# A transformer layer on one core: two loads and three groups of small products moved, and the inverse's equal iterations as a loop on TensorE

## What is computed

```python
q_l = q.reshape(b, H, M, l, DH).sum(axis=3) / l        # M = 64 landmarks
k_l = k.reshape(b, H, M, l, DH).sum(axis=3) / l
attn1 = softmax(q @ k_l^T); attn2 = softmax(q_l @ k_l^T); attn3 = softmax(q_l @ k^T)
z = attn2^T / (max(col) * max(row))                    # Moore-Penrose inverse, 6 iterations
for _ in range(6):
    az = a @ z
    z = 0.25 * z @ (13 * I - az @ (15 * I - az @ (7 * I - az)))
out = attn1 @ z @ (attn3 @ v)
```

## Time and profile before

| | |
|---|---|
| median of 3 runs | 1166.59 us |
| the profiled execution's own time | 1159.38 us |
| its span | 1157.6 us |
| PE busy | 1100.6 us, 95% of the span |
| DVE, ACT, POOL busy | 634.0, 303.0, 300.5 us |
| PE, share of the chain that ended last | 87% |
| PE busy in 300 to 400 us | 85.75 us |
| granted clock of TensorE, mean | 0.99 |
| DMA, mean over the span | 60 GB/s |

### The profile page before, as it was taken

How to read it: one execution, slowest core, us unless ns; L and a number is a source line. 1 busy time by engine, 2 the same in 40 slices (tenths; PEclk the granted TensorE clock), 3 DMA queues, 4 the chain that set the end, 5 groups by cost and what they waited for, 6 DMA issues and landing times.

```text
span 1157.6 us, 22799 instructions
## 1 busy us (share of the span) xinstructions
PE 1100.6 (95%) x9162; PEld 914.3 (79%) x9162; DVE 634.0 (55%) x1346; ACT 303.0 (26%) x457; POOL 300.5 (26%) x298
## 2 busy tenths in 40 slices
PE   4998999999988899999999999889999999999996
PEld 4887888888877756677766777777888888899996
DVE  6467566555467566676686686663332333334442
ACT  4432233332223422342332333231111111111110
POOL 6000000000200013235534544552323323334343
PEclk9999999999999999999999999899999999999999
DMA  9200000000220030211321324145333333231221
GB/s 338 107 1 1 1 1 1 1 1 1 57 77 5 4 146 28 102 55 65 139 65 64 102 74 142 61 135 115 51 52 46 51 52 51 33 48 35 44 27 12
DMA packets 48551, 69.13 MB, mean 60 GB/s; under 512 B 7872, under 2 KB 41792, under 8 KB 47424
## 3 DMA queue, kind: packets, MB, share of 16 engines
q1 hardware_dynamic: 34720, 47.50, 12.9%
q0 software_dynamic: 13296, 16.92, 8.6%
q10 hardware_dynamic: 432, 3.24, 0.7%
HBM read 42.10 MB, written 26.46 MB: 59 GB/s over the span
## 4 chain that ended last, share of the span: by engine, by line
PE 87%; DVE 6%; issue 3%; POOL 2%; ACT 1%; another core or an unknown queue 0%; POOLq 0%; DVEq 0%
PE ps L1712 20%; PE ps L1735 10%; PE ps L1599 10%; PE ps L1375 9%; PE ps L1638 9%; PE ps L1336 9%; PE ps L1630 5%; PE ps L1509 2%; PE ps L1695 1%; PE ps L1618 1%; PE ps L1310 1%; PE ps L1490 1%; PE ps L1477 1%; PE ps L1390 1%; PE ps L1566 1%
## 5 line engine op out<-in xcount | busy, mean ns | idle before, releaser
L1712 PE MATMUL ps<-mem 128*128 128x256 f32 (+1 forms) x1504 | 260.7, 329 | 0.0
L1712 PEld LDWEIGHTS ps<-mem 128*128 128x128 f32 x1504 | 232.7, 191 | 21.5
L565 POOL DMA_INDIRECT out<-mem x71 | 122.9, 1732 | 255.8 <-DVE mem L1215 189.1
L1735 PE MATMUL ps<-mem 128*128 x568 | 135.3, 381 | 5.7 <-DVE mem L1207 3.4
L1207 DVE TENSOR_TENSOR mem<-mem,ps 128x512 f32<-128x512 f32 x71 | 48.8, 687 | 164.6 <-PE ps L1712 143.8
L535 POOL TENSOR_TENSOR mem<-mem,small 128x1024 f32<-128x1024 f32 x36 | 68.6, 1906 | 260.7 <-DVE small L1144 127.8
L1599 PE MATMUL ps<-mem 128*128 128x512 f32 x288 | 129.7, 594 | 1.3 <-DVE mem L1028 1.3
L771 ACT ACTIVATE mem<-ps 128x512 f32<-128x512 f32 x71 | 42.4, 597 | 319.3 <-PE ps L1712 312.8
L1638 PE MATMUL ps<-mem 128*128 128x256 f32 x512 | 120.0, 388 | 0.0
L1375 PE MATMUL ps<-mem 128*128 128x256 f32 x512 | 119.1, 386 | 0.8 <-ACT mem L645 0.8
L1735 PEld LDWEIGHTS ps<-mem 128*128 128x128 f32 x568 | 104.3, 191 | 18.5 <-issue 6.3
(11 more groups left out here) (219 smaller groups left out, 1314.7 us busy)
## 6 DMA issues: line engine op xcount, KB each, us to landing
mem<-w_gu SPq DMA_DIRECT2D x9, 1024.0 KB, 4.3
mem<-xs_d SPq DMA_DIRECT2D x22, 260.0 KB, 2.8
mem<-x SPq DMA_DIRECT2D x8, 512.0 KB, 7.4
mem<-x SPq DMA_DIRECT2D x32, 128.0 KB, 2.1
out<-mem SPq DMA_DIRECT2D x32, 128.0 KB, 1.7
mem<-w_down SPq DMA_DIRECT2D x8, 512.0 KB, 5.1
xnt_d<-mem ACTq DMA_DIRECT2D x3, 1056.0 KB, 5.4
mem<-xnt_d SPq DMA_DIRECT2D x3, 1056.0 KB, 4.9
```

Of the source, the lines that this page charges most:

```text
L565: pool.indirect_dma_start(out=out_rows, out_offset=bass.IndirectOffsetOnAxis(ap=rows[:, D + 1:D + 2].bitcast(U32), axis=0), in_=ys[:, r % ...
L1712: mm = pe.matmul(bank(2 * c + n % 2)[:, i * size:(i + 1) * size], w[:, k, c, f * P:(f + 1) * P], xst[:, a % 2, k, 0:size], start=(k == 0), ...
L1735: mm = pe.matmul(bank(down_bank(a, b))[:, 0:D], hid[:, u, i * size + b * P:i * size + (b + 1) * P], w_d_s[:, e, f], start=(f == 0), stop=( ...
```

## The change

It has four parts.

1. The two moves of loads. `e3s[0]` and `e3s[3]` swap places, so that `wfc` now shares its space with `e3s[0]`, last used at m = 12. SP issues `w_fc` once 13 of the `c1_ut` are done, ahead of the band. `batch_columns(1)` goes behind the gate and up weights of the four experts.
2. The small work of attention 2 is moved to later m, on all three engines: `sim2(2)` and `sim2(3)` with their wait for `b_sub` from m = 1 to 2, `a_transposed` from m = 2 and 3 to 4 and 5, the two sums from m = 5 to 6 and the scale from 7 to 9 (the first sum stays at 4).
3. The 64 first products (line 1456) go from m = 14 to m = 15.
4. PE's part of the inverse: the first pair is written out in `first_pair`, the ten pairs n = 2 to 20 become five trips of a loop in hardware (`pe.Fori`) with two pairs in its body, and the pair n = 22 follows. Counts of semaphores in the loop are register values, so each wait is an instruction of its own (`wait_alone`). Waits that follow from others are left out: a pair now has 5 waits, each an instruction of its own; before, it had 6 such instructions, and four products carried a wait besides. DVE's and ACT's programs for the inverse are as before.

```diff
-        e3s = [at(a, RT * 2 * P).rearrange("p (t c) -> p t c", t=RT) for a in (o + J * D, SQ, wk_at, o)]
+        e3s = [at(a, RT * 2 * P).rearrange("p (t c) -> p t c", t=RT) for a in (o, SQ, wk_at, o + J * D)]
...
+            sp.wait_ge(s("c1_ut"), NP2 - 3)
+            sp.dma_start(wfc, w_fc.rearrange("(j p) c -> p j c", p=P)).then_inc(s("w_in"), 16)
             sp.wait_ge(s("c1_sim"), 2 * NP2)
             sp.dma_start(band, conv_band.rearrange("h p c -> p h c")).then_inc(s("band_in"), 16)
             sp.dma_start(bfc, b_fc.rearrange("(o c) -> o c", o=1).to_broadcast([P, D])).then_inc(s("bfc_in"), 16)
             for m in range(XR):
                 residual_rows(m)
-            sp.wait_ge(s("c1_v3mm"), NP2)
-            sp.dma_start(wfc, w_fc.rearrange("(j p) c -> p j c", p=P)).then_inc(s("w_in"), 16)
             sp.wait_ge(s("a_xnt_out"), 16 * (B - 1))
-            batch_columns(1)
             sp.wait_ge(s("p_wt_mm"), NQ // 4)
             for e in range(4):
                 expert_gate_up(e)
+            batch_columns(1)
...
-                if m == 1:
-                    pe.wait_ge(s("c1_utb"), 1)
+                if m in (2, 4, 5):
+                    pe.wait_ge(s("c1_utb"), m)
+                    pe.wait_ge(s("c1_v3"), 2 * m - 2)
+                if m == 2:
                     sim2(2)
                     sim2(3)
-                if m in (2, 3):
-                    pe.wait_ge(s("c1_utb"), m)
-                    pe.wait_ge(s("c1_v3"), 2 * m - 2)
-                    a_transposed(2 * m - 4)
-                    a_transposed(2 * m - 3)
+                if m in (4, 5):
+                    a_transposed(2 * m - 8)
+                    a_transposed(2 * m - 7)
                 if more:
                     c1_sim(2 * m + 5)
-                if m == 1:
+                if m == 2:
                     pe.wait_ge(s("b_sub"), B)
-                if m in (2, 3):
-                    pe.wait_ge(s("b_at_act"), m - 1)
-                    pe.wait_ge(s("b_at_dve"), m - 1)
-                if m == NP2 - 2:
+                if m in (4, 5):
+                    pe.wait_ge(s("b_at_act"), m - 3)
+                    pe.wait_ge(s("b_at_dve"), m - 3)
+                if m == NP2 - 1:
                     pe.wait_ge(s("c1_raw"), 2 * NP2)
...
-            for n in range(0, 4 * ITERS, 2):
+            def first_pair():
+                for k in range(2):
+                    pe.wait_ge(s("i_yw"), k + 1)
+                    for i in range(8):
+                        mm = square(k, i)
+                    mm.then_inc(s("i_squaremm"), 1)
+                c1_v3(NP2 - 1)
+                for k in range(2):
+                    pe.wait_ge(s("i_br"), k + 1)
+                    if k == 0:
+                        pe.wait_ge(s("i_yw"), 4)
+                    for i in range(8):
+                        mm = cube(k, i)
+                    mm.then_inc(s("i_cubemm"), 1)
+
+            def pair(n, done):
+
                 for k in range(4):
-                    if n == 0 and k == 2:
-                        c1_v3(NP2 - 1)
-                    (square_ready if k < 2 else cube_ready)(n + k % 2)
-                    if n >= 2 and k % 2 == 0:
-                        next_ready(n - 2 + k // 2)
+                    if k < 2:
+                        wait_alone(pe, "i_yw", done + n + k + 1)
+                        if k == 0:
+                            wait_alone(pe, "i_factor", done + n - 1)
+                    else:
+                        wait_alone(pe, "i_br", done + n + k - 1)
                     for i in range(8):
                         mm = (square if k < 2 else cube)(n + k % 2, i)
-                        if n >= 2:
-                            crossed = next_values(n - 2 + k // 2, 8 * (k % 2) + i)
+                        crossed = next_values(n - 2 + k // 2, 8 * (k % 2) + i)
                     mm.then_inc(s("i_squaremm" if k < 2 else "i_cubemm"), 1)
-                    if n >= 2 and k % 2 == 1:
+                    if k % 2 == 1:
                         crossed.then_inc(s("i_nextmm"), 1)
+
+            first_pair()
+            pe.wait_ge(s("i_w0"), 1)
+            pe.wait_ge(s("c1_r3"), NP2)
+            pe.wait_ge(s("c1_v3"), NQ)
+            with pe.Fori(0, ITERS - 1) as it:
+                pair(2, 4 * it)
+                pair(4, 4 * it)
+            pair(4 * ITERS - 2, 0)
```

More of the change, by code:

```diff
@@ L672, in _ @@
                     c1_raw(2 * m + 4)
-                if m == 1:
+                if m == 2:
                     sim2_exp(2)
                     sim2_exp(3)
-                if m in (2, 3):
-                    b = 2 * (m - 2)
+                if m in (4, 5):
+                    b = 2 * (m - 4)
                     act.wait_ge(s("b_at_tp"), b + 1)
@@ L949, in _ @@
                     c1_first_max(m + 2)
-                if m == 1:
+                if m == 2:
                     sim2_less_max(2)
                     sim2_less_max(3)
-                if m in (2, 3):
-                    b = 2 * (m - 2) + 1
+                if m in (4, 5):
+                    b = 2 * (m - 4) + 1
                     dve.wait_ge(s("b_at_tp"), b + 1)
@@ L970, in _ @@
                     dve.tensor_reduce(zz[:, 0:1], mx2, AX, ALU.max).then_inc(s("b_sums"), 1)
-                if m == 5:
+                if m == 6:
                     dve.wait_ge(s("b_at_dve"), 2)
@@ L975, in _ @@
                     dve.tensor_reduce(zz[:, 1:2], sm2s, AX, ALU.max).then_inc(s("b_sums"), 1)
-                if m == 7:
+                if m == 9:
                     dve.wait_ge(s("b_gmax"), 1)
```

## The result

| | before | change |
|---|---|---|
| median, first comparison | 1167.37 us (1164.97 to 1168.68, 4 runs) | 1151.8 us (1146.11 to 1153.58, 4 runs) |
| ratio of medians | | 0.9865, interval 0.9836 to 0.9893 |
| median, second comparison, another chip (`e10` below) | 1159.23 us (11 runs) | 1145.87 us (1144.63 to 1146.23, 4 runs) |
| ratio | | 0.9882, interval 0.9858 to 0.9906 |

The change is faster, by 15.6 us in one comparison and 13.4 in the other; both intervals lie clear of 1. The forecast was 12.8. In the profiled execution of the changed kernel (1153.58 us) the gain is smaller, 5.8 us of 1159.4. Where the rest was lost is shown further down.

What follows compares the result with a forecast made beforehand. PE bounds the kernel, and in the inverse the arrival of its instructions does. Terms -4.0 - 0.75 - 2.8 - 5.2 = -12.8 us: 1146.6 from the profiled 1159.4, 1153.8 against the median 1166.6; 8-in-10 range 1148 to 1182.

Steps and rivals of the forecast that it cites:

- `sim2` to m = 2: First stage, m == 1: removes PE's 4.0 us wait at line 1365, with some 1.5 us new idling at `c1_max_columns(3)`; -4.0 us.
- gone: 5.20 - 3.65 of slow matmuls after it: First stage, m == 1: the 16 matmuls after the removed stall return to usual speed, 1.55 us won.
- `a_transposed`: First stage, m == 2, 3 to 4, 5: same PE work where PE has no gap, copies fit others' idling; 0.
- First products: End of first stage, line 1456: moved to m == 15, the 64 products fill PE's wait for bank 6; -0.75 us.
- they cover it: End of first stage: the products' 3.88 us hide the 0.75 us wait for bank 6 between two `c1_ut`.
- Loads: Inverse: earlier `w_fc` and later columns remove the 3.09 us stall (-2.3) and slow matmuls after it (-0.5); -2.8 us.
- The loop: Inverse: kept instruction blocks spare fetch stalls, 1.1 us a trip over four trips plus one stall of 0.8; -5.2 us.
- The next bound: Inverse loop: VectorE at 8.3 us a trip limits the gain to 3.0 us a trip, -12 in all.
- Rival A: Inverse loop: branch finds its target gone, four blocks fetched each trip, 15.8 us instead of 11.3; 1179 us, chance 0.33.
- Rival B: Inverse loop: blocks are fetched again at each edge, pace stays 3.6 us a block, only moves count; 1159 us, chance 0.12.
- rival C: Moves give nothing (4 us wait returns at `c1_max_columns(3)`), register steps eat the loop's gain; 1163 to 1167 us, chance 0.05.
- What was to be seen: Signs: 4 or 5 loop packets, not 14; copies 9.6 to 10.4 us per four; no 3 us inverse stall.

Runs made afterwards that it cites:

- e10: The changed kernel itself, unaltered, timed again on another chip beside the kernel before: 1145.87 us, ratio 0.9882.
- e4: The changed kernel with `sim2(2)`, `sim2(3)` and the wait for `b_sub` back at m = 1, on all engines: one run, 1148.6 us against 1159.5 before.
- e1: The changed kernel with the inverse written out as before, so the moves without the loop: 1153.73 us against 1159.9 before, ratio 0.9948.
- e6: The changed kernel with `w_fc` and the columns of batch 1 loaded where they were before: one run, 1148.06 us.
- e7: The changed kernel with four pairs in the loop's body, two trips, and two pairs written out behind it: one run, 1147.57 us.
- e5: The changed kernel with the 64 first products back at m = 14: one run, 1144.14 us.
- e8: The changed kernel with six pairs in the loop's body, two trips, and seven iterations of the inverse instead of six (two pairs more work): 1171.15 us.
- e2: The changed kernel with the same pairs and 5 waits a pair, written out by a Python loop instead of the hardware loop: 1156.37 us, ratio 0.9972 to before.
- e9: The changed kernel with half of `c1_ut(1)` ahead of `c1_max_columns(3)`, and at m = 2 the scores ahead of `c1_max_rows(3)`: 1145.5 us, ratio 0.9881 to before.
- e11: The same kernel as e9, timed again beside the changed kernel on one chip: 1147.04 us, ratio 0.9892 to before.
- e3: The kernel before with the hardware loop alone, no moves: 1151.6 us, ratio 0.9927 to before.

## Why the prediction was right, term by term

The forecast was -12.8 us. The marks give -11.9 (the change) and -12.7 (e10) at the start of the landmark values, the medians -13.4 and -15.6. The terms are less good than the sum, whose closeness is in part luck: the two terms in c1 were 2.4 us too large together (4.75 for 2.3) and the loop's about 2.6 too small.

1. **`sim2` to m = 2: forecast -4.0.** e4 against the change at m = 6 gives -1.9. The stall that takes its place was foreseen at the right instruction and nearly in size (1.9 us for 1.5; the forecast's own terms, 95.79 + 2 + 1 + 1.83, come to 100.6 and not to its 100.2, and would have given 1.8). What failed is the step "gone: 5.20 - 3.65 of slow matmuls after it". In the change the group after the new stall is as slow, 5.14 us, as it follows 1.9 us of idling. But it need not be. The chain of e1, the same program up to there, after the same stall:

```profile
99.89 0.44 DVE mem L873
...
100.81 3.46 PE ps L1375 x16
```

The granted clock in 102:106 is 0.65 in the change (busy row below) and 1.00 in e1, e6 and e7.

```profile
102.00:106.00 4.00, 4.00 (x14) 3.19 (x14) 1.79 (x3) 0.00 (x0) 0.00 (x0) 0.65 0.00 0
```

Of the eight profiled executions with this c1 or e5's (the same up to m = 14), four have the slow group (change, e5, e8, e10) and four have not (e1, e2, e6, e7), and with it the inverse starts at 317.1 to 317.4 us, without it at 315.5 to 315.6. So the term is -1.9 or -3.6. That one program can go both ways, none of these eight shows: the change itself had the slow group both times. The nearest evidence is e9 and e11, one program with the same wait and two different clocks after it.

2. **`a_transposed`: forecast 0.** Within the 0.44 us of e4.

3. **First products: forecast -0.75, measured -0.2.** The step "they cover it" was right for the wait at m = 15 and forgot the one at m = 14, that they had covered until then. The earlier trace rows showed the products standing in front of that wait; I read this as a wait that needed no cover.

4. **Loads: forecast -2.8.** e6 gives 2.8 to 4.1 in the inverse with the loop, e1 1.8 in the written-out one. The stall goes as foreseen (3.09 us before; in e1's chain none exceeds 0.98 up to 380 us); the size holds within 1.3 us either way.

5. **The loop: forecast -5.2, measured about -8** (e1's inverse 71.87 us, the change's 64.08). The mechanism was right and the size was not. Written out, three trips' worth takes 33.48 us, 11.16 each (forecast 11.3); in the loop a trip takes 9.31 (forecast 9.8 and 0.4 for register steps and the branch, 10.2). The branch costs the pace nothing: the first square behind it starts 0.3 us late (4.95 us after the pair before it, where 4.66 is usual), the pair makes that up, and e7, with half as many branches, has the same 4.66 us a pair. The register steps have no run of their own; they lie within the 0.6 us per trip in which PE isn't busy. Four trips of 1.85 us are 7.4. The next bound was to be VectorE with 8.3 us a trip. VectorE is busy 7.74 us of a trip and PE 8.73, so by these busy times PE's own products are the nearest bound. The chain runs through the round trip of a pair, 4.66 us from PE to ScalarE's copy to VectorE to PE, but a shorter round trip could win no more than PE's 0.6 us.

**Rival A** (the branch finds its target gone) is a true mechanism, and nearly of the size given. e8 shows it: a stall of 4.2 us at the branch, and then the pace of straight code (33.8 us for six pairs, written out 33.48). That is some 4 us per trip above straight code; the forecast had 15.8 - 11.3 = 4.5. Its condition, that fewer than four blocks are kept, isn't met: the store keeps eight, and the change needs four and the one behind them. What held 0.33 for it was that no row of before shows a branch. **Rival B** falls by the 40 us without a packet, **rival C** by e3 and e1.

What was to be seen: 4 or 5 packets in the loop (four, the first of them 0.9 us ahead of its first product), copies at 9.6 to 10.4 us per two pairs (9.31, faster than that), 1 to 2 us of idling at `c1_max_columns(3)` (1.9), no 3 us stall in the inverse (longest 1.31 in the chain, 1.36 behind the loop).

## What to carry to other kernels

Where a stage is made of small products and the chain shows "issue" stalls at equal distances of one packet of the instruction queue, the instructions are the bound: fewer waits don't help (e2), a hardware loop whose body stays in the store does (e7, not e8). A large load issued into such a stage delays the very packet that it needs; issue it a stage earlier. And a wait for another engine's result can move on to the next product when the order changes (e9), so price the next late one before crediting the first.

## What was not expected of the hardware

- TensorE's instruction store keeps eight blocks of 256 instructions (e7) and not eleven (e8), though it fetches only one ahead; with a body inside it, neither the branch nor the register steps of a trip are to be seen in the pace (4.66 us a pair with two pairs or four in the body).
- A branch to a block that is gone cost 4.2 us once, little more than one of the 3.4 to 4 us turns of straight code.
- After the same stall of 1.9 us, in programs alike up to there, the granted clock dropped in four executions (0.61 to 0.68 over 102:106, the group 5.14 us) and not in four others (1.00, 3.46 us). After the same wait of 3.1 us one program had 0.57 over 114:122 in e9 and 0.79 in e11, and its inverse started at 319.77 and 318.36 us. A stall of 1.9 us had a price of 0 or 1.7 us.
- Counts that PE's products give came 7 to 8 us after the products in one execution and within 0.02 us of them in another of the same program.
